# One kernel of four engine streams: a written-out call list per engine, a PSUM bank per product from a table, and Silu taken from ScalarE's table

## The reference, cut to what matters

```python
# 1. bidirectional decayed scan per channel (twice: weights w,u and w2,u2 over the same S)
a_t = a_{t-1} * decay + exp(S_t) * S_t        # forward and, reversed, backward
b_t = b_{t-1} * decay + exp(S_t)
base = sigmoid(r) * (nf + nb - ekv + e^u ek v) / max(df + db - ek + e^u ek, 1e-8)
# 2. state-space attention on the first one
z, xc, B, C, dt = split(base @ in_proj_w)      # 256 -> 512+512+64+64+8
v = silu(causal_conv(xc)); B, C = elu(B)+1, elu(C)+1
y = chunked_decay_attention(C, B, v, exp(-softplus(dt+bias)*exp(A_log))) + D*v
x = x + (rmsnorm(y) * silu(z)) @ out_proj_w
# 3. feed-forward on the second one (r = x)
h = quant(rms(base2)) @ tern(w1).T + b1        # 256 -> 1024
h = layer_norm(gelu(silu(h))) * g + b
x = x + quant(rms(h)) @ tern(w2).T + b2        # 1024 -> 256
```

## Time and profile before

| | us |
|---|---|
| median of 3 runs | 280.08 (280.02 to 280.82) |
| the profiled execution, its time | 280.92 |
| its span, first to last instruction | 278.9 |
| DVE busy | 199.3 (71% of the span) |
| ACT busy | 173.4 (62%) |
| PE busy | 163.2 (59%) |
| POOL busy | 148.5 (53%) |

### The profile page before, as it was taken

One profiled execution on the slowest core, in us unless ns is written; L12 is line 12 of the kernel. 1 busy time (PEld: TensorE's weight loads), 2 busy tenths in 40 slices (PEclk: granted clock), 3 DMA queues, 4 the chain that ended last, 5 costly groups with the idle time before them and its releaser, 6 DMA issues.

```text
span 278.9 us, 2545 instructions
## 1 busy us (share of the span) xinstructions
PE 163.2 (59%) x690; PEld 109.5 (39%) x690; DVE 199.3 (71%) x290; ACT 173.4 (62%) x290; POOL 148.5 (53%) x154
## 2 busy tenths in 40 slices
PE   0000567407599349797029988899848545434464
PEld 0000445106178226476005745766626324222242
DVE  0699759997259998377997637842697786988653
ACT  3707496149947129986007848637569696688861
POOL 2630086910554920425684144544387789999950
PEclk9999999955759958999656999999995955975579
DMA  5994002002000000000000000000000000000001
GB/s 169 420 373 152 0 5 70 1 1 75 0 2 0 0 0 0 0 2 1 0 1 0 0 4 0 0 0 0 2 0 0 0 1 4 19 19 20 19 19 56
DMA packets 5501, 10.02 MB, mean 36 GB/s; under 512 B 752, under 2 KB 3568, under 8 KB 5232
## 3 DMA queue, kind: packets, MB, share of 16 engines
q1 hardware_dynamic: 5056, 9.71, 9.6%
q10 hardware_dynamic: 432, 0.16, 0.4%
HBM read 8.82 MB, written 1.05 MB: 35 GB/s over the span
## 4 chain that ended last, share of the span: by engine, by line
DVE 22%; PE 20%; ACT 20%; POOL 18%; issue 16%; DMA 2%; ACTq 0%; POOLq 0%; DVEq 0%
PE banks L1294 18%; DVE Fs L919 7%; DVE nd L937 5%; DVE Ys L925 3%; POOL wn L496 3%; ACT D L585 3%; PE banks L1291 3%; POOL own L471 3%; POOL gmv L425 2%; DMA condb<-in_cond_dram 2%; POOL Fs L471 2%; ACT dec L675 2%; POOL grs L427 1%; ACT L845 1%; ACT Ys L602 1%
## 5 line engine op out<-in xcount | busy, mean ns | idle before, releaser
L406 POOL TENSOR_TENSOR dv<-vv,heads 128x512 f32<-128x512 f32 x8 | 8.3, 1042 | 44.6 <-ACT vv L663 44.6
L919 DVE TENSOR_TENSOR_SCAN Fs<-D,E 128x1028 f32<-128x1028 f32 x8 | 22.8, 2874 | 5.5 <-POOL E L372 5.4
L1294 PE MATMUL banks<-uT,inw 128*128 128x256 f32 x80 | 24.6, 463 | 2.1 <-DVE bcf L1024 2.1
L1294 PE MATMUL banks<-inw,uT 128*128 128x8 f32 (+1 forms) x64 | 25.0, 533 | 0.0
L394 POOL TENSOR_TENSOR dec<-tri,la 128x1024 f32<-128x1024 f32 x8 | 21.5, 2697 | 2.6 <-DVE la L1059 2.5
L1291 PE MATMUL banks<-ident,wn 128*128 128x128 f32 x64 | 12.3, 354 | 17.8 <-POOL wn L496 16.7
L1294 PE MATMUL banks<-dec,late 128*128 128x512 f32 x32 | 18.2, 703 | 6.3 <-ACT dec L675 5.7
L925 DVE TENSOR_TENSOR_SCAN Ys<-D,Fs 128x1028 f32<-128x1028 f32 x8 | 21.3, 2698 | 0.0
L1294 PEld LDWEIGHTS banks<-uT,inw 128*128 128x128 f32 x80 | 18.0, 234 | 6.5 <-DVE bcf L1024 2.8
L1037 DVE SCALAR_TENSOR_TENSOR cv<-banks,cols,cv 128x255 f32<-128x255 f32 (+2 forms) x48 | 19.1, 471 | 0.9 <-ACT cv L636 0.9
L1294 PE MATMUL banks<-w2T,yzT 128*128 128x256 bf16 x64 | 12.4, 340 | 10.7 <-ACT yzT L789 10.7
(11 more groups left out here) (166 smaller groups left out, 513.8 us busy)
## 6 DMA issues: line engine op xcount, KB each, us to landing
wn<-in_w_dram SPq DMA_DIRECT2D x2, 1024.0 KB, 11.1
inw<-in_in_w_dram SPq DMA_DIRECT2D x1, 1160.0 KB, 8.3
vT<-in_kT_dram SPq DMA_DIRECT2D x4, 256.0 KB, 9.8
xcT<-in_xT_dram SPq DMA_DIRECT2D x4, 256.0 KB, 10.5
xn<-in_x_dram SPq DMA_DIRECT2D x4, 256.0 KB, 8.8
out_dram<-ot SPq DMA_DIRECT2D x8, 128.0 KB, 1.7
outw<-in_out_w_dram SPq DMA_DIRECT2D x1, 512.0 KB, 12.1
lnbb<-in_ln_b_dram SPq DMA_DIRECT2D x1, 512.0 KB, 8.6
```

The costliest lines, as they stand in the source:

```text
L406: pool.tensor_tensor(by_head(dv[:, c]), by_head(vv[:, b % 2, c]), heads[:, 2, :].unsqueeze(2).broadcast_to([P, NH, HD]), ALU.mult).then_in ...
L919: dve.tensor_tensor_scan(Fs[:, w], D[:, w, 0:L], E[:, b % 2].rearrange("p k c t -> p (k c t)"), 0.0, ALU.mult, ALU.add).then_inc(fs_ok, 1)
L1294: return pe.matmul(dst, lhsT, rhs, start=start, stop=stop)
```

## The change

The computation is the same but for the order of some factors. The change has six parts.

1. The loops over `b` and `ffn_step` are gone. Each engine has one list of calls, written out: 87 calls on POOL, 122 on PE, 191 on DVE, 171 on ACT (3 of them issue a DMA) plus 28 table loads, 28 on SP. PE's list also has bare waits between calls.
2. `HOME` gives each product a bank of its own choice; waits by bank are gone where the list's order implies them. `decays` works on one bank (512 columns) instead of two.
3. Silu comes from ACT's table: `ffn_silu` moves from DVE to ACT and replaces Tanh. Gelu has no scale.
4. ACT's multiplication by the reciprocal deviation and POOL's addition of the bias are gone; DVE makes `lnbb * std + Y` (`ffn_shift`), `std` comes from POOL as one more column, and the reciprocal deviation goes into the scale of ACT's squaring and into the small factors (`gq`, `qfl`).
5. The sum over the conditioning vector is a PE product with ones over a transposed 64 x 4 input, in place of a broadcast load of 128 KB and a DVE reduction.
6. The order of the loads changes, `starts` is bf16, `U` and `Q2` lie in `wn`, the square outputs have buffers of their own.

```diff
+HOME = {
+    "cond_sum": 0,
+    "weight_sums": 1,
+    "features": (2, 1, 6, 2),
...
+    "ffn_up": ((3, 6), (5, 2), (7, 3), (4, 7), (6, 4), (3, 7), (1, 4), (5, 6)),
+    "ffn_turns": ((0, 1), (6, 4), (6, 3), (7, 4), (5, 0), (2, 1), (7, 4), (0, 6)),
+    "ffn_down": (0, 2, 1, 3, 6, 5, 3, 2),
+}
...
+        def at(name, *part):
+            home = HOME[name]
+            for k in part:
+                home = home[k]
+            return banks[:, home, :]
...
# GpSimd: the deviation keeps std; the bias is gone
+            def ffn_dev(i):
+                s = slice(i, i + 1)
+                pool.wait_ge(gvar_ok, i + 1)
+                rsqrt(gmv[:, s], grs[:, s], 1, gvar[:, s], gmv_ok, grs_ok, i + 1, 1.0 / NI, EPS)
+                pool.wait_ge(grs_ok, i + 1)
+                pool.tensor_scalar(std[:, s], gmv[:, s], grs[:, s], 1.0, ALU.mult, ALU.mult).then_inc(std_ok, 1)
-            def ffn_bias(i):
-
-                pool.wait_ge(Yr_ok, i + 1)
-                pool.wait_ge(ln_in, 48)
-                pool.tensor_tensor(y_row(i), y_row(i), lnbb[:], ALU.add).then_inc(Y_ok, 1)
...
# ScalarE
+            def ffn_silu(i):
+                act.wait_ge(U_ok, 2 * (i + 1))
+                act.activation(U[:, i % 2], U[:, i % 2], ACT.Silu).then_inc(S_ok, 1)
...
-                act.activation(TH, U[:, i % 2], ACT.Tanh, scale=0.5).then_inc(TH_ok, 1)
-                act.activation(y_row(i), y_row(i), ACT.Copy, scale=grs[:, i:i + 1]).then_inc(Yr_ok, 1)
+                act.activation(junk_q[:], Y[:, i % 2], ACT.Square, scale=grs[:, i:i + 1], accum_out=qss[:, i:i + 1])\
+                    .then_inc(qss_ok, 1)
...
# VectorE
-                dve.scalar_tensor_tensor(U[:, i % 2], TH, 1.0, U[:, i % 2], ALU.add, ALU.mult).then_inc(S_ok, 1)
+            def ffn_shift(i):
+                dve.wait_ge(std_ok, i + 1)
+                dve.wait_ge(W_ok, i + 1)
+                dve.wait_ge(lnb_in, 16)
+                dve.scalar_tensor_tensor(Y[:, i % 2], lnbb, std[:, i:i + 1], Y[:, i % 2], ALU.mult, ALU.add)\
+                    .then_inc(Y_ok, 1)
...
# TensorE: conditioning sum
+                mm(at("cond_sum")[:, 0:B], ones[0:TE, :], condc[:], True, True).then_inc(cs_ps, 1)
```

More of the change, by code:

```diff
@@ L322, in _ @@
[L322 to L331 removed]
+            load_k(3)
+            load_inw()
@@ L547, in _ @@
[L547 to L551 removed]
+            first_turn()
+            make_ident()
+            own_times_v(1)
+            make_late()
+            times_v(1)
+            second_ratio(0)
+            log_decays(0, 0)
+            scale_outw()
+            times_v(2)
+            log_decays(0, 1)
+            state_values(0)
+            skip_term(0, 0)
+            skip_term(0, 1)
@@ L1280, in _ @@
-            residual(LAST)
-            ffn_in(LAST)
-            ffn_in_max(LAST)
-            ffn_step(3)
-            for k in range(4, NT + 4):
-                ffn_step(k)
+            make_ones()
+            wkv_min(0)
+            decay_factor()
+            make_pads()
+            make_decay()
+            make_gap()
+            own_min(0)
+            first_D()
+            own_min(1)
+            forward(0, 0)
+            forward(0, 1)
+            backward(0, 0)
+            wkv_min(1)
@@ new lines, in _ @@
+            add_own(0, 0)
+            backward(0, 1)
+            out_factor()
+            add_own(0, 1)
+            recip(0, 0, 1)
+            wkv_min(2)
+            ratio(0)
+            recip(0, 1, 2)
+            gated(0)
+            forward(1, 0)
+            forward(1, 1)
+            softplus_in(0)
+            backward(1, 0)
+            backward(1, 1)
+            softplus_out(0)
+            add_own(1, 0)
+            add_own(1, 1)
+            weight_mean()
+            conv_taps(0, 1)
@@ new lines, in _ @@
+            features(0)
+            conv_taps(0, 0)
+            recip(1, 0, 2)
+            own_min(2)
+            wkv_min(3)
+            ratio(1)
+            mask_scores(0)
+            attend(0, 0)
+            forward(2, 0)
+            gated(1)
+            forward(2, 1)
+            softplus_in(1)
+            y_scale(0)
+            norm_gate(0, 0)
+            attend(0, 1)
+            softplus_out(1)
+            backward(2, 0)
+            backward(2, 1)
+            norm_gate(0, 1)
@@ new lines, in _ @@
+            features(1)
+            clip_weights(0)
+            add_own(2, 0)
+            add_own(2, 1)
+            conv_taps(1, 1)
+            residual(0)
+            conv_taps(1, 0)
+            ffn_in(0)
+            recip(2, 0, 2)
+            ratio(2)
+            gated(2)
+            ffn_in_max(0)
+            ffn_in_scale(0)
+            ffn_in_back(0)
+            mask_scores(1)
+            softplus_in(2)
+            attend(1, 0)
+            own_min(3)
+            clip_weights(1)
@@ new lines, in _ @@
+            y_scale(1)
+            features(2)
+            attend(1, 1)
+            ffn_u(0, 0)
+            norm_gate(1, 0)
+            forward(3, 0)
+            ffn_u(0, 1)
+            norm_gate(1, 1)
+            forward(3, 1)
+            backward(3, 0)
+            backward(3, 1)
+            residual(1)
+            add_own(3, 0)
+            ffn_in(1)
+            softplus_out(2)
+            add_own(3, 1)
+            conv_taps(2, 1)
+            conv_taps(2, 0)
+            recip(3, 0, 2)
@@ new lines, in _ @@
+            ffn_mean(0)
+            mask_scores(2)
+            attend(2, 0)
+            ffn_in_max(1)
+            y_scale(2)
+            ffn_in_scale(1)
+            attend(2, 1)
+            ffn_in_back(1)
+            ffn_u(1, 0)
+            norm_gate(2, 0)
+            ffn_center(0)
+            ffn_u(1, 1)
+            norm_gate(2, 1)
+            ffn_u(2, 0)
+            ffn_u(2, 1)
+            ratio(3)
+            gated(3)
+            ffn_shift(0)
+            residual(2)
+            ffn_mean(1)
@@ new lines, in _ @@
+            ffn_center(1)
+            ffn_in(2)
+            ffn_max(0)
+            ffn_in_max(2)
+            ffn_u(3, 0)
+            ffn_scale(0)
+            softplus_in(3)
+            ffn_mean(2)
+            ffn_in_scale(2)
+            features(3)
+            softplus_out(3)
+            conv_taps(3, 1)
+            conv_taps(3, 0)
+            ffn_u(3, 1)
+            ffn_shift(1)
+            mask_scores(3)
+            ffn_in_back(2)
+            attend(3, 0)
+            ffn_u(4, 0)
```

1611 lines of the change are left out of this document (883 added, 728 removed).

## The result

The median is 226.97 us (225.89 to 227.94, 4 runs) against 280.05 for the kernel before in the same session: ratio 0.810, 95% interval 0.806 to 0.814. I had said 239, with 228 to 256. The sign was right, the size was 12 us off, and the value lies 1 us under the low end of the range.

What follows compares the result with a forecast made beforehand. No engine was full, so the order was taken to cost, with POOL bounding the end. The pieces 32 + 63 + 95 + 46 = 236, plus 2 for hops and contention, gave a span of 238, standing for 239 us; range 228 to 256.

Steps and rivals of the forecast that it cites:

- No engine is full, so it is the order that costs: Whole kernel before: DVE busy 71%, ACT 62%, PE 59%, POOL 53%; the gain, if any, is in the order.
- Start, 28.7 becomes 32: Start to the end of `gated(0)`: first scan at about 12.7 us, mark at 32, 3.5 us later than before.
- Second piece, 63: End of `gated(0)` to end of `gated(2)`: 83.3 us becomes 63, DVE calls summing to 61 plus about 2 of waiting.
- Third piece: End of `gated(2)` to end of `residual(3)`: 106.5 us becomes 95 by walking the lists; sums ACT 88, PE 91, DVE 80.
- Last piece, 46: End of `residual(3)` to the end: 60.5 us becomes 46, bound by ACT at 38.4 less 2, plus waits and last output.
- 2 us for hops and contention on top: Added to the whole walk's 236 us for semaphore hops and contention beyond average, giving a span of 238.
- A table switch costs 1.28 and no more: On ACT, each table switch costs its 1.28 us load, without the further 1.38 us drain of the Trainium skill's rule.
- Rival C: Table switches bound ACT: 0.6 us more on each of 20 loads, 251 us, chance 0.06; at 1.38, 267, chance 0.01.
- B, the dense piece gets no busier: Between `gated(2)` and `residual(3)` DVE stays 0.675 busy, so 119 us instead of 95; time 263 us, chance 0.14.
- D, PE's list: PE's fixed list of 122 calls, through its banks, holds all streams; the kernel gets slower, 285 us, chance 0.03.
- Busy times: Whole kernel after the change: DVE busy 196 us (82% of the span), ACT 174, POOL 139.
- POOL not at the end of the chain: In the last 45 us POOL, at 6.1 us a row tile, is no longer the bound; ACT is over 80% busy.

Runs made afterwards that it cites:

- tail2: The changed kernel with Silu of rows 6 and 7 behind one table load (two loads fewer) and last-piece calls reordered to match: 226.72 us, ratio 0.806 to 0.811.
- more_loads: The changed kernel with eight more table loads on ACT, each ahead of an existing one, between the ends of `gated(2)` and `residual(3)`: 234.49 us, ratio 0.832 to 0.838.
- old_shift_silu: The kernel before in its own order, with old_shift's normalisation algebra and Silu from ACT's table in place of Tanh and DVE's product: 287.24 us, ratio 1.020 to 1.026.
- old_shift: The kernel before in its own order, with only the FFN normalisation algebra changed (`ffn_shift` replaces ACT's scaling and POOL's bias): 282.27 us, ratio 1.004 to 1.007.
- new_tanh: The changed kernel with Tanh and the product on DVE back in place of the table's Silu, and six fewer table loads: 236.18 us.

## Why the prediction was right in sign and 12 us too high

- *No engine is full, so it is the order that costs.* Right: the whole change gives 19%, its arithmetic in the old order +2.3%. That it is the order, and not the bank table or the smaller parts that came with it, is not shown.
- *Start, 28.7 becomes 32.* 33.8. First scan said 12.7, measured 14.0: the pow took 3.46 instead of 3.10 and started at 7.36. Both causes that I named (`first_turn` behind `own_times_v(0)`, the second chain ahead of the first seed) are there. I did not count the second product, under which `backward(0, 0)` takes 4.38.
- *Second piece, 63.* 62.7, but by two errors that cancel: the call sum was 61, the durations sum to 65.5 (scans and `add_own` beside POOL's products), and overlap takes that to 60.3 busy.
- *Third piece, "106.5 becomes 95".* This is the step that failed, and in it a size: the work sums "ACT 88, PE 91, DVE 80", on which the walk ran. The walk let each call start when the one before had ended. Along DVE's stream my 95 is 80 of work and 15 of waits; measured are 71.5 of work and 11.7 of waits, together 83.2. So 8.5 of the 11.8 us lie in the work term and 3.3 in the waits (the 3.57 ahead of `softplus_in(2)` I had called 3). The durations of DVE's instructions do add up to 80.3; neighbours overlap by 0.07 us on average, 8.8 in all. For ACT the durations add up to 83.9, with 13 loads and 67.2 of calls where I had 14 and 70, and 9.2 of overlap leaves 74.7. PE's 91 measured 77.0: the piece of before has 81.8 busy for 377 products at a clock of 0.89, which for the 386 here would be 83.8, and an estimated 77.6 at the granted 0.96. So the clock explains about 6 of the 14; the other 7 were too much in my sum. The low end of the range stood on the same sum: 228 took this piece at ACT's 88 as its least. That it was the overlap which moved the mark is argued from these sums; no run takes it away.
- *Last piece, 46.* 45.3. I had taken ACT as its bound (38.4 less 2; measured 34.8, 77% busy, where I wanted over 80). tail2 shows that ACT is not it. That the sum came out right is luck: the chain of this piece lies half on POOL, which I had called "no longer the bound", in small instructions that I had put at 0.26 each.
- *2 us for hops and contention on top.* Not needed: the walk's missing overlap was larger than both.
- *A table switch costs 1.28 and no more.* Right. In the changed kernel all 28 loads start within 0.03 of the end of the instruction before; behind 23 the next one starts within 0.02, behind four the rows name another engine that ACT waits for, and behind the first there are 0.16. more_loads shows the same. Rival C falls, with both its prices.
- *B, the dense piece gets no busier.* Wrong: DVE went from 67.5% to 86%. *D, PE's list.* It did not cost 41 us, but the idea behind it, that four fixed lists hold one another, is what the costs of an added microsecond on DVE and PE suggest.
- *Busy times:* DVE said 196, measured 190.0; ACT 174 and 173.5; POOL 139 and 149.4. POOL's one-column instructions were put at 0.26; `std`, `stdf` and `gq` took 0.26, 0.74 and 0.35, 10.8 us instead of 6.2, and their price depends on what DVE does beside them (below).
- *POOL not at the end of the chain.* Wrong: it has the largest share, 15%.

## What to carry to other kernels

Add up starts, not durations: take an engine's busy time over the sum of its durations in the trace at hand (before the change 0.90 for ACT, 0.92 for DVE) and scale a walk by it. Here that would have made DVE's 80 about 74 and the piece about 89, half of the way to 83. Don't carry the clock of the old order over either: it was 0.89 where PE was 77% busy and 0.96 where it was 93% busy.

In this kernel of fixed streams, with three engines near 90%, a microsecond added to DVE or PE cost nearly a microsecond, while 4 us taken from DVE, or a wait moved, gave nothing. Look for the next wait on the same engine, and at what a neighbour runs at the new time, before promising a gain. And a change of arithmetic is worth what the order around it lets through: Silu from the table in place of Tanh made the kernel 1.8% slower in the old order (old_shift_silu against old_shift), while in the new one going back to Tanh made it 2 to 4% slower (the shortest run and the median of new_tanh against the changed kernel).
